# Strassen products for the down projection of the first token half, with the weight forms stored for the second

## The reference

```python
x = _layernorm(x + _L0_attn_ref(x, wq, wk, wv, wo))          # x: 4 x 512 tokens of 1024
gate_w = gate_t.astype(f32) * gate_s[:, None]                # 3584 x 1024, entries -1, 0, 1
up_w   = up_t.astype(f32) * up_s[:, None]
down_w = down_t.astype(f32) * down_s[:, None]                # 1024 x 3584
hidden = silu(x_flat @ gate_w.T) * (x_flat @ up_w.T)
x = _layernorm(x + hidden @ down_w.T)
```

## Time and profile before

| what | value |
|---|---|
| median of three runs | 1866.86 us |
| profiled execution, whole | 1868.12 us |
| its span on the core | 1866.4 us |
| granted TensorE clock, mean over the span | 0.993 of full speed |
| TensorE busy | 1807.0 us, 97% |
| VectorE busy | 1187.7 us, 64% |
| ScalarE busy | 710.5 us, 38% |
| GpSimd busy | 543.6 us, 29% |
| mean DMA traffic | 125 GB/s |

### The profile page before, as it was taken

One profiled execution on the slowest core, in us unless ns is written; L12 is line 12 of the kernel. 1 busy time (PEld: TensorE's weight loads), 2 busy tenths in 40 slices (PEclk: granted clock), 3 DMA queues, 4 the chain that ended last, 5 costly groups with the idle time before them and its releaser, 6 DMA issues.

```text
span 1866.4 us, 27364 instructions
## 1 busy us (share of the span) xinstructions
PE 1807.0 (97%) x10528; PEld 882.0 (47%) x10528; DVE 1187.7 (64%) x2047; ACT 710.5 (38%) x1112; POOL 543.6 (29%) x845
## 2 busy tenths in 40 slices
PE   7889999999999998999999999999999999999997
PEld 4545655555555543444444444444444444444443
DVE  7877778668768764445544444745656765667645
ACT  5443444444434444436433343342232322222221
POOL 1354546456546564131000000211321211112103
PEclk9999999999999999999999999999999999999999
DMA  8543234334334398557644353649321211232301
GB/s 246 118 103 78 54 85 125 83 80 116 90 52 114 81 212 221 209 208 263 236 171 150 107 195 126 215 148 211 127 66 53 79 66 51 72 104 85 107 12 79
DMA packets 228162, 233.13 MB, mean 125 GB/s; under 512 B 183872, under 2 KB 184128, under 8 KB 228032
## 3 DMA queue, kind: packets, MB, share of 16 engines
q1 hardware_dynamic: 227168, 230.99, 42.2%
q10 hardware_dynamic: 864, 0.39, 0.1%
HBM read 122.55 MB, written 72.88 MB: 105 GB/s over the span
## 4 chain that ended last, share of the span: by engine, by line
PE 85%; DVE 6%; issue 3%; SPq 2%; POOL 2%; ACT 1%; DMA 1%; ACTq 0%; DVEq 0%; POOLq 0%
PE bank L1053 31%; PE bank L948 20%; PE bank L1074 13%; PE bank L1087 6%; PE bank L998 4%; PE bank L960 3%; PE bank L984 3%; PE bank L1013 2%; SPq L1587 2%; DVE down_forms L1391 1%; PE bank L963 1%; DVE gate_blocks L1385 1%; POOL p_tiles L1451 1%; DVE row_max L1267 0%; DVE up_blocks L1375 0%
## 5 line engine op out<-in xcount | busy, mean ns | idle before, releaser
L1053 PE MATMUL bank<-x_forms,weight_forms 128*128 128x512 f16 x3136 | 700.9, 379 | 12.7 <-DVE gate_blocks L1375 4.4
L1053 PEld LDWEIGHTS bank<-x_forms,weight_forms 128*128 128x128 f16 x3136 | 305.3, 98 | 387.0 <-DVE gate_blocks L1375 7.1
L1139 ACT ACTIVATE p_tiles<-bank 128x512 f32<-128x512 f32 (+1 forms) x352 | 193.0, 556 | 276.6 <-PE bank L984 273.5
L1267 DVE TENSOR_REDUCE row_max<-bank 128x1 f32<-128x384 f32 (+3 forms) x352 | 220.0, 636 | 98.2 <-PE bank L963 96.6
L1074 PE MATMUL bank<-down_forms 128*128 128x512 f16 x1152 | 259.6, 381 | 2.4 <-issue 2.4
L948 PE MATMUL bank<-wq_parts,xT_parts 128*128 128x256 f16 x1536 | 219.4, 275 | 8.9 <-DVE wq_parts L1231 8.7
L1410 DVE TENSOR_TENSOR acc<-bank,acc 128x512 f32<-128x512 f32 x188 | 127.6, 687 | 124.2 <-PE bank L1074 64.7
L1443 POOL TENSOR_SCALAR_AFFINE_SELECT p_tiles<-p_tiles 128x128 f32<-128x128 f32 (+2 forms) x352 | 139.0, 403 | 212.2 <-ACT p_tiles L1139 210.9
L1074 PEld LDWEIGHTS bank<-down_forms 128*128 128x128 f16 x1152 | 113.0, 98 | 139.7 <-issue 4.9
L948 PEld LDWEIGHTS bank<-wq_parts,xT_parts 128*128 128x128 f16 x1536 | 144.1, 98 | 56.8 <-issue 14.2
L948 PE MATMUL bank<-wo_parts,att_parts 128*128 128x512 f16 x672 | 170.1, 382 | 0.6 <-DMA att_parts<-att_spill 0.6
(11 more groups left out here) (114 smaller groups left out, 1999.9 us busy)
## 6 DMA issues: line engine op xcount, KB each, us to landing
weight_forms_spill<-weight_forms SPq DMA_DIRECT2D x28, 896.0 KB, 5.7
weight_forms<-weight_forms_spill SPq DMA_DIRECT2D x28, 896.0 KB, 4.5
x_forms_spill<-x_parts SPq DMA_DIRECT2D x56, 256.0 KB, 2.4
w_page<-gateT SPq DMA_DIRECT2D x28, 512.0 KB, 5.0
w_page<-upT SPq DMA_DIRECT2D x28, 512.0 KB, 4.0
w_page<-downT SPq DMA_DIRECT2D x28, 512.0 KB, 4.3
att_spill<-att_made SPq DMA_DIRECT2D x64, 128.0 KB, 2.1
down_forms<-x_spill SPq DMA_DIRECT2D x16, 512.0 KB, 3.4
```

Source lines behind the costliest of these rows:

```text
L1053: t = nc.tensor.matmul(strassen[bank_set(use)][to][:, :], w_form[:, use % 4, A_FORMS[a_form], k * P:(k + 1) * P], xF[:, :, B_FORMS[b_form] ...
L1139: nc.scalar.activation(p32[j][:, h0:h0 + heads, :], bank[5 + m % 2][:, 0:heads * n].rearrange("p (h c) -> p h c", c=n), ACT.Exp, scale=SCO ...
L1267: nc.vector.tensor_reduce(mx[:, u % 2, i, h0:h0 + ROW_HEADS[i]], bank[3 + m % 2][:, 0:ROW_HEADS[i] * n].rearrange("p (h c) -> p h c", c=n) ...
```

## The change

Rounds 0 to 9 of the first pass get the seven forms too; rounds 10 to 13 stay plain. The four forms of the down weights are made by VectorE in the first pass, straight after the cast. What goes to DRAM is then all seven (896 KB in place of 512 KB for each of those ten rounds), and the second pass loads all seven and has no `d_form`. Because rounds 0 to 9 use three places in place of four, round n of the first pass now waits for round n-3 (`room_after`, and the stores of those places, `stored_before`). The output scale `ds` and the rows `x1_row` lie inside the form region 1; in the first pass they are now loaded only after group 3 of down is done, as in the second pass. The first down product waits for the last hidden block of round 1, whose up product used its bank.

```diff
-DOWNS = [(q, m) for q in range(PASSES * ND) for m in range(PAIRS * NPR if ND <= q < PASSES * ND - 1 else 2 * PT)]
+DOWNS = [(q, m) for q in range(PASSES * ND) for m in range(PAIRS * NPR if q % ND < ND - 1 else 2 * PT)]
 def plain(n):
-    return n < NF or n % NF >= PLAIN
+    return n % NF >= PLAIN
 def room_after(n):
     p, r = divmod(n, NF)
-    if p == 0:
-        return DOWN_OF[r - 4] if r > 3 else None
-    return DOWN_OF[p * NF + min(r - 3, PLAIN - 1)] if r > 2 else p * ND - 1
+    if r > 2:
+        return DOWN_OF[p * NF + min(r - 3, PLAIN - 1)]
+    return p * ND - 1 if p else None
+def stored_before(r):
+    return [] if r < 3 else [r - 3] if r < NF - 1 else [r - 5, r - 4]
...
-            for _ in range(4 if n < NF else 10):
+            for _ in range(10):
                 if left and DOWN_ROUNDS[left[0][0]][-1] < n:
                     down_at[left.pop(0)] = clock
-                    clock += one if n < NF else one / 2
+                    clock += one / 2
...
+        room += [("d_store", r) for r in stored_before(n)] if n < NF else []
...
-            [("down", *DOWNS[d - 1])] if d else [("att_scale", NU - 1, UG - 1)]) + ...
+            [("down", *DOWNS[d - 1])] if d else [("att_scale", NU - 1, UG - 1), ("hidden", 1, 3)]) + ...
...
-        put(SY, at, .4, "ds_load", p, moves=PAGE_MOVES, after=over + ([("down", *DOWN_LAST[p * ND + ND - 3]), ("acc", *DOWN_LAST[p * ND - 1])] if p else []))
+        put(SY, at, .4, "ds_load", p, moves=PAGE_MOVES, after=over + [("down", *DOWN_LAST[p * ND + ND - 3])] + (
+            [("acc", *DOWN_LAST[p * ND - 1])] if p else [("d_store", PLAIN - 3)]))
...
         if w == 2 and c == 1:
-            put(SY, at + 6, .4, "d_store", r, moves=PAGE_MOVES, after=[("w_cast", w, r, 0), ("w_cast", w, r, 1)])
+            if not plain(r):
+                for k, form in enumerate(DOWN_MADE):
+                    put(VE, at + 2 + .5 * k, .45, "d_form", r, form, after=[("w_cast", w, r, 0), ("w_cast", w, r, 1)] + (
+                        [("d_form", r, DOWN_MADE[k - 1])] if k else []))
+            put(SY, at + 6, .4, "d_store", r, moves=PAGE_MOVES if plain(r) else FORMS_MOVE / 2, after=[
+                ("w_cast", w, r, 0), ("w_cast", w, r, 1)] if plain(r) else [("d_form", r, DOWN_MADE[-1])])
...
-        if not plain(n):
-            for k, form in enumerate(DOWN_MADE):
-                put(VE, at + 6 + .5 * k, .45, "d_form", n, form, after=[("d_in", n)] + ([("d_form", n, DOWN_MADE[k - 1])] if k else []))
...
-    wd_dram = nc.dram_tensor("w_down_spill", [NF, P, 2 * D], F16, kind="Internal").ap()
+    wd_dram = nc.dram_tensor("w_down_spill", [NF, P, NPR * HALF], F16, kind="Internal").ap()
...
                 elif kind == "w_cast":
...
                         projections_over(on)
                         place_free(on, r)
-                        on.wait_ge(s_dst[r % 4], 16 * (r // 4))
-                        to = wd_p[place_of(r)][:, c, :]
+                        to = wd_p[place_of(r)][:, c, :] if plain(r) else wd_f[r % 3][:, 2 * c:2 * c + 2, :].rearrange("p f c -> p (f c)")
```

More of the change, by code:

```diff
@@ L558, in ffn_plan @@
             after = [("hid_lo", r, a_form) for r in rounds]
-            after += [("d_form", r, b_form) if b_form in DOWN_MADE else ("d_in", r) for r in rounds]
+            if p:
+                after += [("d_in", r) for r in rounds]
+            else:
+                after += [w for r in rounds for w in (
+                    [("d_form", r, b_form)] if b_form in DOWN_MADE else [("w_cast", 2, r, int(b_form != "B11"))])]
         else:
@@ L563, in ffn_plan @@
         put(PE, at + 5, one * len(rounds) / (2 if plain(rounds[0]) else 4), "down", q, m, after=after + (
-            [("down", *DOWNS[d - 1])] if d else [("att_scale", NU - 1, UG - 1)]) + ([("acc", *DOWNS[d - 2])] if d > 1 else []))
+            [("down", *DOWNS[d - 1])] if d else [("att_scale", NU - 1, UG - 1), ("hidden", 1, 3)]) + ([("acc", *DOWNS[d - 2])] if d > 1 else []))
         room = [("acc", *DOWNS[d - 1])] if d else []
@@ L574, in ffn_plan @@
             put(PO, at + one + 1, 2.4, "scale_row", tile, after=[("acc", q, m), ("ds_scale", p)])
-            put(SY, at + one, .4, "last_x1", tile, moves=PAGE_MOVES, after=over + ([("down", *DOWN_LAST[q - 1])] if p else []) + (
+            put(SY, at + one, .4, "last_x1", tile, moves=PAGE_MOVES, after=over + [("down", *DOWN_LAST[q - 1])] + (
+                [] if p else [("d_store", PLAIN - 3)]) + (
                 [("add_x1", tile - 1)] if tile else []))
@@ L596, in ffn_plan @@
         if w == 2:
-            room = outputs + ([("down", *DOWN_LAST[DOWN_OF[r - 4]]), ("d_store", r - 4)] if r > 3 else [])
+            room = outputs + ([("down", *DOWN_LAST[room_after(r)])] if r > 2 else []) + [("d_store", o) for o in stored_before(r)]
         put(SC, at, 1.06, "w_cast", w, r, c, after=[("w_load", w, r, c)] + room + ([("w_cast", *pages[i - 1])] if i else []))
@@ L610, in ffn_plan @@
         at, old = use_at[2 * n + 1] - 6, room_after(n)
[L611 removed]
+        put(SY, at, .4, "d_in", n, moves=PAGE_MOVES if plain(n) else FORMS_MOVE / 2, after=[("d_store", n - NF), ("down", *DOWN_LAST[old])] + (
             [("acc", *DOWN_LAST[old])] if old == ND - 1 else []))
[L613 to L615 removed]
     for m, (p, form, pair) in enumerate(FORM_LOADS):
@@ L1062, in tensor_program @@
                     on.wait_ge(s_scale_att, 4 * NU * UG)
+                    on.wait_ge(s_hid, 8)
                     if plain(rounds[0]):
@@ L1362, in vector_program @@
                     n, form = which
-                    b = wd_f[n % NF % 3]
-                    on.wait_ge(s_din[(n - NF) % 4], 16 * din_n(n))
+                    b = wd_f[n % 3]
+                    for c in range(2):
+                        on.wait_ge(s_cast, cast_n["w_cast", 2, n, c])
                     on.wait_ge(s_dform, dform_n["d_form", n, form] - 1)
```

34 lines of the change are left out of this document (23 added, 11 removed).

## The result

Four runs of the changed kernel gave 1891.2, 1894.18, 1894.58 and 1894.92 us, median 1894.38, against 1866.94 for the kernel before in the same job: a ratio of 1.013 (95% interval 1.0111 to 1.0148). It is slower by 1.3%. The prediction was 1869.6 us, with a range up to 1877, so the result lies 25 us above the forecast and outside the range.

The account below looks back on a forecast made before the run. TensorE alone was taken to bound the first pass, with room on VectorE. Savings of 17.3 us against added waits summed to +2.7 us on the median of 1866.86, giving 1869.6 us, range 1861 to 1877.

Parts of the forecast that it names:

- Removed: First pass, five down groups by forms: 80 matmuls fewer, 17.3 us saved, all on the path.
- Round 3 into 4: First pass, behind the run of group 0's last 19 products: TensorE loses 5.4 us to cast, splits and gate sum.
- Round 2 into 3: First pass, no down product between: 2.7 us for the chain plus 1.5 for a late start, 4.2 lost.
- Round 1 into 2: First pass: 1.3 us lost, between 0 and 2.5, including a layer norm split and late weight forms.
- Round 9 into 10: First pass: 3.4 us lost, of which 1.4 from `ds` loaded late and scaled ahead of the last up sum.
- The other changes of round: First pass, two to ten down products between: 2.8 us lost in all, between 0 and 6.
- The x1 additions: First pass, rows of x1 now added in rounds 10 to 12: 1.0 us lost, between 0 and 1.4.
- Second pass: `d_form` leaves, first down products of groups 7 to 9 move behind the third gate product: 1.9 us lost.
- two a round: First pass: about two VectorE operations a round held by GpSimd, 1.1 us each, 21 us over ten rounds.
- Late pages: Rival: ScalarE's pages arrive late after the run of 80 matmuls, first pass; +7.7, 1874.5 us; chance 0.35.
- Covered: Rival: most changes of round stay covered, only 9.5 us lost, 7.8 gained, 1859 us; chance 0.25.
- three signs of being wrong: First pass: idle behind the run under 3 us; none at round 2 into 3; new form or cast waits over 3.

Follow-up runs that it names:

- e1: Changed kernel plus 84 extra matmuls, result unread, ahead of seven TensorE waits; 1885.69 us, ratio 1.0086 to the kernel before.
- e7: Changed kernel moving 512 KB of down weights per store and load, no `d_form` in the second pass; 1896.4 us, ratio 1.0148.
- e6: Changed kernel storing and loading 512 KB per round, with VectorE making the four down forms again in the second pass; 1893.92 us, ratio 1.0132.
- e4: Changed kernel with rounds 0 to 3 of the first pass plain, in four places, saving 48 matmuls; 1881.49 us, ratio 1.0057.
- e5: Changed kernel with each round's first gate sum and gate copy moved ahead of splits and weight forms in the order; 1875.34 us, ratio 1.0034.
- e8: Kernel before the change, with each round's first gate sum and gate copy moved ahead in the order; 1873.69 us, ratio 1.0029.
- e9: Changed kernel with hidden forms on VectorE, gate sum ahead at rounds 3, 4 and 10, and 60 filler matmuls; 1877.1 us, ratio 1.005.
- e10: Kernel before the change, with hidden forms on VectorE and 8 filler matmuls in one wait; 1865.65 us, ratio 0.9987.
- e12: As e9 on the changed kernel, but 16 filler matmuls in place of 60; 1875.15 us, ratio 1.0047.

## Why the prediction was wrong

**What failed: each wait was priced at its idle time.** In "The changes of round, one by one" and in the sum there is no term for the clock. The row it was taken from, 2.69 us at 1359.87, had cost nothing beyond itself; I took that for the rule, although the wait of 2.44 us near the end of the same trace had cost 1.5 us more. The same wait of 2.69 at 1381.59 did cost 1.7 us more, and e1 gave back about 8 us by filling. In profiled times the miss is 26.1 - 2.7 = 23.4 us; the clock is 10.5 of it, waits longer than their terms 8.7 (28.7 - 20.0), and 3.5 the last point of the list below. That is 22.7; 0.7 is not placed.

**The sizes of the waits**, measured against the term, in the order of the prediction:
- Removed: 17.3 us, right; the count fell by 80.
- Round 3 into 4: 5.4 predicted, 2.01 + 3.56 = 5.57 measured, by the chain that was described.
- Round 2 into 3: 4.2, measured 5.42. A split of layer norm rows on ScalarE waited 1.86 us for a store, which I had not seen; without the larger transfers it waited 1.10 (e7), and TensorE's wait is 4.53 and 4.54 (e6, e7).
- Round 1 into 2: 1.3, measured 1.8 (1.77, 0.33, 0.51, 0.25 and 1.20, less the 0.80, 1.11 and 0.34 of before).
- Round 9 into 10: 3.4, measured 3.21, but not by its parts. VectorE did not wait for `down_s`: `ds_scale` began at 1159.19 straight behind an `acc`. The four `d_form` took 2.73 us, a `hid_lo` 1.75 and a `w_form` 1.50, beside GpSimd. The number is right by luck: the 1.4 us of a late `ds` weren't there, and held instructions filled the gap.
- The other changes of round: 2.8, measured 5.9: 2.20 at 0 into 1 in place of 0.5, where the `hid_lo` of GpSimd's first form, which VectorE waited 1.16 us to begin, and a layer norm split of 1.75 us (0.67 before) stood ahead of the sum; 1.59 and 1.60 at 5 into 6 and 7 into 8 in place of 0.5; 0.51 at 4 into 5; none at 6 into 7 and 8 into 9.
- The x1 additions: 1.0, measured 3.9. The 1.36 at 1242.46 was the one I had priced; 0.94, 1.39 and 0.16 before down products, which wait for `acc`, came on top. A `hid_lo` took 2.31 us and two `w_form` 3.03 there.
- Second pass: 1.9, measured 3.5 (13.8 against 10.3 us). The step named was right for the gate products behind the down products (1.31, 0.96, 0.96 and 1.66 in place of 0.37 three times and 0.63). The 0.38 at 1339.76 did not go: it is 0.69 at 1358.03, for a gate copy on ScalarE. Ahead of the second pass a wait for `x_forms` is 0.55 shorter.
- Not in the sum: 0.163 us that each further wait costs beside what it shows, 2.6; and 0.9 at the out-projections.

So the mechanism was right at most places, and the sizes were small where I had only an estimate by feel: 0 into 1, 5 into 6, 7 into 8, the x1 additions. Held instructions stand at the first and the last of these (at the x1 additions beside two additions on GpSimd of 5.1 us together, whose hold I had not counted): I let the rows that show 1.75 us stand for two a round, while the sentence beside it, by which `w_form` and `d_form` are held too, described what then happened (1.50 for one `w_form` at 1162.54, 2.73 for four `d_form` at 1166.30). And no sum or `acc`, which read PSUM, took over 0.70 us.

**The rivals.** Late pages had the sign and 0.35; its mechanism is refuted by e7 and by the new waits for weight forms or casts, none over 0.33 us. "Covered" is refuted by 28.7 us of new waits where it had 9.5. No case had the slow side beyond 1874.5, and the range ended at 1877 although the high ends of the terms made 1880. The low ends add to 7.0 us and 1856.6, not 8 and 1857.5. None of the three signs of being wrong came, though the result was 25 us off: they tested where the waits would stand, and none tested their sum or the clock. One forecast that could have shown it failed: the second pass was to start at the same distance from the beginning, and the product behind the wait of 2.69 us starts 21.7 us later (1381.59 against 1359.87).

**What stays open.** Why the clock fell behind 2.69 us in one kernel and not in the other, and behind 2.15 us at 828.19 but not behind 2.16 at 824.34 before. The wait of 2.44 us near the end is the cleanest case: behind it 20 matmuls take 5.8 to 6.0 us in eight of the 14 profiles and 4.3 in six (e4, e5, e8, e9, e10, e12), so its length alone doesn't decide it. Whether e12's fills would have been worth more at another size. I did not try a down group 0 that starts earlier, which would take the run of 80 apart.
